# Two normalised tiles per batch go from VectorE to ScalarE in the two routers of an audio tower

## The reference

```python
def _layernorm(x, axis=-1, eps=1e-05):
    m = jnp.mean(x, axis=axis, keepdims=True)
    v = jnp.var(x, axis=axis, keepdims=True)
    return (x - m) / jnp.sqrt(v + eps)
# first mixture
S = jax.nn.softmax(x @ Wg, axis=-1)          # x = layernorm(h), Wg 128 x 8
# second mixture
logits = t @ gate_w.T + gate_b
probs = jax.nn.softmax(logits, axis=-1)
h = h + _L0_ffn_ref(_layernorm(h, axis=-1), ...)
h = h + _L1_ffn_ref(_layernorm(h, axis=-1), ...)
```

## Time and profile before

| what | value |
|---|---|
| median of 3 runs | 3237.22 us (3235.11 to 3238.65) |
| profiled execution | 3239.33 us |
| its span | 3237.6 us |
| busy PE, DVE, ACT, POOL | 2806.1, 2397.2, 1872.4, 1005.0 us |
| mean granted TensorE clock | 0.932 of full speed |

### The profile page before, as it was taken

How to read it: one execution, slowest core, us unless ns; L and a number is a source line. 1 busy time by engine, 2 the same in 40 slices (tenths; PEclk the granted TensorE clock), 3 DMA queues, 4 the chain that set the end, 5 groups by cost and what they waited for, 6 DMA issues and landing times. The chain is left out here.

```text
span 3237.6 us, 56270 instructions
## 1 busy us (share of the span) xinstructions
PE 2806.1 (87%) x16922; PEld 2239.5 (69%) x16922; DVE 2397.2 (74%) x4399; ACT 1872.4 (58%) x3098; POOL 1005.0 (31%) x873
## 2 busy tenths in 40 slices
PE   8975999999999999419999999588855899799994
PEld 8975665665666665319999999488844688688883
DVE  4544888888888886778999999377738666578775
ACT  3343466666666666308888888144422677577773
POOL 0033000000000000204555555233302577466664
PEclk9988899999999999759999999699967899899997
DMA  1138444355344341002322222220040211277767
GB/s 51 33 141 275 60 67 61 49 64 62 51 60 65 52 56 23 27 15 77 91 84 86 85 86 90 88 99 0 0 169 2 89 48 48 91 239 245 241 192 228
DMA packets 149262, 290.48 MB, mean 90 GB/s; under 512 B 23006, under 2 KB 77981, under 8 KB 142220
## 3 DMA queue, kind: packets, MB, share of 16 engines
q1 hardware_dynamic: 135564, 264.13, 33.4%
q0 software_dynamic: 13568, 24.75, 2.3%
HBM read 203.15 MB, written 87.11 MB: 90 GB/s over the span
## 5 line engine op out<-in xcount | busy, mean ns | idle before, releaser
L840 DVE TENSOR_REDUCE part_max<-to_dve 128x1 f32<-128x374 f32 (+1 forms) x1536 | 744.0, 540 | 163.3 <-PE to_dve L750 148.6
L902 ACT ACTIVATE probs<-score 128x748 f32<-128x748 f32 x768 | 579.7, 794 | 403.9 <-PE score L770 402.5
L750 PE MATMUL to_dve<-k_stack,q_stack 127*128 127x374 f32 (+1 forms) x1536 | 509.7, 377 | 30.9 <-DMA k_stack<-k_parts 30.8
L750 PEld LDWEIGHTS to_dve<-k_stack,q_stack 127*128 127x128 f32 (+1 forms) x1536 | 272.7, 190 | 299.6 <-DVE part_max L840 252.4
L2460 DVE TENSOR_TENSOR m_hid_lo<-m_hid,m_hid_hi 128x512 fp32r<-128x512 f32 x408 | 289.8, 711 | 161.3 <-ACT m_hid_hi L2433 161.3
L770 PE MATMUL score<-q_stack,k_stack 128*128 128x374 f32 x1536 | 395.1, 339 | 0.0
L1357 DVE TENSOR_TENSOR f_hid_lo_c<-f_hid_c,f_hid_hi_c 128x748 fp32r<-128x748 f32 x256 | 350.0, 1376 | 42.6 <-ACT f_hid_hi_c L1340 39.6
L680 POOL TENSOR_TENSOR h<-h,o_rows 128x256 f32 (+2 forms) x96 | 49.4, 531 | 944.9 <-DVE o_rows L863 944.9
L1253 POOL TENSOR_TENSOR f_acc_c<-f_acc_c,f_gate_c 128x748 f32<-128x748 f32 x112 | 253.1, 2259 | 259.6 <-DVE f_gate_c L1373 259.3
L786 PE MATMUL o_sum<-probs,v_sb 128*17 128x374 f32 (+1 forms) x3072 | 315.9, 483 | 16.4 <-ACT o_cols L893 14.0
L1335 ACT ACTIVATE f_hid_c<-f_up_c,c_b 128x374 f32<-128x374 f32 x512 | 268.5, 571 | 76.3 <-DVE f_hid_lo_c L1357 52.0
(11 more groups left out here) (412 smaller groups left out, 6170.9 us busy)
## 6 DMA issues: line engine op xcount, KB each, us to landing
m_weights<-e_records SPq DMA_DIRECT2D x54, 1028.0 KB, 6.8
f_gate_c<-c_gates SPq DMA_DIRECT2D x128, 374.0 KB, 3.4
q_stack<-q_parts SPq DMA_DIRECT2D x128, 187.0 KB, 5.4
k_stack<-k_parts SPq DMA_DIRECT2D x128, 187.0 KB, 9.4
e_slots<-blank SPq DMA_DIRECT2D x54, 260.0 KB, 3.6
m_row_in<-e_slots SPq DMA_DIRECT2D x54, 260.0 KB, 3.0
m_weights<-e_sums SPq DMA_DIRECT2D x16, 640.0 KB
e_records<-rec_parts SPq DMA_DIRECT2D x16, 512.0 KB, 3.9
```

What stands on the lines that cost most here:

```text
L750: last = pe.matmul(ring[bank][0:ROWS[c], 0:HALF], q_stack[its_slot][0:MAX_ROW, head, c * P:c * P + ROWS[c]], k_stack[its_slot][0:MAX_ROW, ...
L840: dve.tensor_reduce(part_max[0:ROWS[c], head, c, half:half + 1], ring[bank][0:ROWS[c], 0:HALF], AX.X, ALU.max).then_inc(used, 1)
L902: act.activation(probs[:, s % 2, head, :, :], score[e % 2][:, :, 0:HALF], ACT.Exp).then_inc(prob_done, 1)
```

## The change

`OWN`, the number of tiles per batch that DVE normalises, goes from 4 to 2. ScalarE makes tiles 2 and 3 with one `activation` of kind Identity each, whose scale is the token's `rstd` and whose bias is a new `shift` = -mean * rstd. The `shift` of all 96 tiles is one more DVE instruction at the end of `weights_and_statistics` (L205), in all four calls. PE's `turn_rows(b)` has one wait more, for `act_ready`. POOL's part is as before.

```diff
@@ weights_and_statistics, DVE
-                dve.reciprocal(g.rstd[:, :], std[:, :])
+                dve.reciprocal(g.rstd[:, :], std[:, :]).then_inc(sums_done, 1)
+                dve.wait_ge(sums_done, 4)
+                dve.scalar_tensor_tensor(out=g.shift[:, :], in0=g.mean[:, :], scalar=-1.0, in1=g.rstd[:, :],
+                                         op0=ALU.mult, op1=ALU.mult)
@@ router_logits
-        OWN = 4
-        centred, pool_ready = sem("r_centred"), sem("r_pool_ready")
+        OWN, SHIFTED = 2, 4
+        centred, pool_ready, act_ready = sem("r_centred"), sem("r_pool_ready"), sem("r_act_ready")
...
-                    tiles = slice(b * TILES + OWN, (b + 1) * TILES)
-                    out = rows_of(b)[:, OWN:TILES, :]
+                    tiles = slice(b * TILES + SHIFTED, (b + 1) * TILES)
+                    out = rows_of(b)[:, SHIFTED:TILES, :]
...
                 def turn_rows(b):
                     pe.wait_ge(ready, b + 1)
                     pe.wait_ge(pool_ready, b + 1)
+                    pe.wait_ge(act_ready, b + 1)
...
             @block.scalar
             def _(act):
+                def norm(b):
+                    if b >= 2 and keep is None:
+                        act.wait_ge(turned, b - 1)
+                    for c in range(OWN, SHIFTED):
+                        at = b * TILES + c
+                        last = act.activation(rows_of(b)[:, c, :], g.h[:, at, :], ACT.Identity,
+                                              bias=g.shift[:, at:at + 1], scale=g.rstd[:, at:at + 1])
+                    last.then_inc(act_ready, 1)
+
+                norm(0)
+                norm(1)
                 for b in range(B):
                     act.wait_ge(turned, b + 1)
                     if b >= 2:
                         act.wait_ge(done, b - 1)
                     round_cols(act, y_hi[:, b % 2, :], turn[b % 2]).then_inc(rounded, 1)
+                    if b < B - 2:
+                        norm(b + 2)
```

More of the change, by code:

```diff
@@ L956, in _ @@
                         pool.wait_ge(turned, b - 1)
-                    tiles = slice(b * TILES + OWN, (b + 1) * TILES)
-                    out = rows_of(b)[:, OWN:TILES, :]
+                    tiles = slice(b * TILES + SHIFTED, (b + 1) * TILES)
+                    out = rows_of(b)[:, SHIFTED:TILES, :]
                     pool.tensor_tensor(out, g.h[:, tiles, :], g.mean[:, tiles].unsqueeze(2).broadcast_to(
-                        [P, TILES - OWN, P]), ALU.subtract).then_inc(centred, 1)
+                        [P, TILES - SHIFTED, P]), ALU.subtract).then_inc(centred, 1)
                     pool.wait_ge(centred, b + 1)
-                    pool.tensor_tensor(out, out, g.rstd[:, tiles].unsqueeze(2).broadcast_to([P, TILES - OWN, P]),
+                    pool.tensor_tensor(out, out, g.rstd[:, tiles].unsqueeze(2).broadcast_to([P, TILES - SHIFTED, P]),
                                        ALU.mult).then_inc(pool_ready, 1)
@@ L2557, in audio_tower @@
         g.rstd = ctx.enter_context(nc.sbuf_tensor("rstd", [P, B * TILES], F32))
+        g.shift = ctx.enter_context(nc.sbuf_tensor("shift", [P, B * TILES], F32))
         g.stats = ctx.enter_context(nc.sbuf_tensor("stats", [P, B * TILES, 6], F32))
```

## The result

The change makes the kernel faster by 0.28%: 3227.60 us is the median of 12 runs (3224.76 to 3229.71) against 3235.93 us of 12 runs of the kernel before (3233.57 to 3238.71); the ratio is 0.9972, 95% interval 0.9965 to 0.9980, so 6.5 to 11.3 us less. The forecast was 3227.5 us. That the two agree to 0.1 us is partly luck: the forecast took 9.7 us from a median of 3237.22, which three runs gave, and twelve runs of the same kernel have 3235.93; the medians differ by 8.3 us.

A forecast was written before the change was run, and what follows sets the result against it. DVE, its norms held up by POOL, was taken to bound the routers, with a 1.94 us loop behind it. The terms -7.2 - 3.7 + 1.2 = -9.7 us, against 3237.22, gave 3227.5 us, range 3225.2 to 3231.6.

The forecast's parts named there:

- What bounds it: Both routers: DVE sets the pace, 2.667 us a batch in router c, its norms held up by POOL's instructions.
- A loop of 1.94 us: Routers, behind DVE: two batches through PE, ScalarE and DVE take 3.88 us, so no period under 1.94.
- four pieces: The loop's 3.88 us: split to PE 1.06, transposes 0.84, rounding 0.88, the rest 1.10 for the matmuls.
- Router c, -7.2 us: Router c: with two norms on DVE, periods of 1.95 us from batch 4 on; last split 7.2 us earlier.
- Router e, -3.7 us: Router e: periods of 2.05 us while POOL works, then 1.95; 3.7 us less, bounds 3.0 to 4.1.
- The shift, +1.2 us: Four statistics blocks: one more DVE instruction on the path, 0.3 us each, 1.2 us more (0.9 to 1.6).
- ScalarE's work at nothing: Both routers: two activations per batch, 0.45 us each, fall where ScalarE idles and cost nothing.
- The limit of 1.09 us for the activations: Routers: ScalarE's next rounding comes late only once the pair of activations takes 1.09 us (1.94 - 0.85).
- Rival 1: Both routers: POOL's hold-ups stay and DVE remains the bound, period 2.23; -5.7 us, 3231.5 us; 14%.
- Rival 2: Routers: ScalarE takes DVE's place if a pair exceeds 1.09 us; at 0.9 for one, 3238.4 us; 5%.
- Rivals 3 and 4: Routers: PE's clock falls, 3261 us, 2%; or the loop gives way too, -11 to -12.5 us, 5%.
- rival 4: Routers: the fast clock may come a batch earlier, or waits shorten, -11 to -12.5 us; 5%.

The follow-up runs named there:

- c_no_pool_before: Kernel before, with POOL leaving out its two tiles in router c from batch 2 on; router c 38.7 us, router e 42.9 us.
- c_no_pool_after: Changed kernel, with POOL leaving out its tiles in router c from batch 2 on; router c 39.7 us, periods 1.70 and 2.21 in turn.
- ring3: Changed kernel with three buffers, norms of batch b+3 behind batch b, PE's transposes of b+2 ahead of matmuls of b; routers 34.2 and 35.6 us.
- after_again: Changed kernel itself, unchanged, timed again on another chip; ratio 0.9968 to the kernel before, routers 39.2 and 38.8 us.
- own1: Changed kernel with one tile per batch on DVE and three on ScalarE; routers 38.2 and 38.6 us.
- own0: Changed kernel with no tile on DVE and all four on ScalarE; routers 41.7 and 41.6 us, period 2.27 us.
- own3: Changed kernel with three tiles on DVE and one on ScalarE; routers 44.1 and 41.1 us, period 2.41 us in router c.
- late_clear: Changed kernel with POOL's five clears moved behind its first two batches; both routers 37.7 us.

## Why the prediction was right, point by point

*What bounds it.* DVE, lengthened by hold-ups, in front: confirmed by `c_no_pool_before` (1.95 with four norms). A loop of 1.94 us behind it: confirmed by `c_no_pool_after` (3.91 for two batches, DVE idle in both, without any hold-up) and `ring3` (1.72 when the loop is opened). The prediction read 3.88 us for two batches; measured 3.91. Of its four pieces the last, 1.10 for the matmuls, was only what was left over, so that they add up is no test.

*Router c, -7.2 us.* Measured -7.86. The eleven periods behind batch 4 were 1.95 each as forecast. The rest is in the first four batches: `split` of batch 4 stood 14.8 us into the router, and the forecast had 15.4. The fast clock came earlier. PE's matmuls of the changed kernel at the change of levels:

```profile
1349.02 0.51 PE L987 MATMUL r_sums_c<-r_hi_c,c_wg_lo 128*128 128x374 f32 x1
1349.33 1.35 PE L212 MATMUL r_turn_c<-ident,r_rows_c 128*128 128x128 f32 x6
1350.46 0.41 PE L987 MATMUL r_sums_c<-r_hi_c,c_wg_hi 128*128 128x374 f32 x1
1350.71 0.33 PE L987 MATMUL r_sums_c<-r_lo_c,c_wg_hi 128*128 128x374 f32 x1
```

The last slow matmul (0.51 us) starts 8.1 us into the router; before it was at 1350.00, 11.3 us in. This is no property of the change that I can show: in `after_again`, the same kernel, the last slow matmul starts 11.0 us in, `split` of batch 3 came at 13.2 us instead of 12.9 and that of batch 4 at 15.4 as forecast, and router c took 39.2 us instead of 38.6. Against 46.4 that is the forecast's 7.2 less; so the 0.7 us more of the first trace look like scatter.

*Router e, -3.7 us.* Measured -4.04. The step that was off is the period beside a working POOL, 2.05 forecast and 1.95 measured: from batch 3 on two norms there took 0.89 to 1.04 us, not 1.14, and the loop hides that. (The bound of -4.1 for 1.94 throughout should read -4.2: 2452.2 + 12 x 1.94 = 2475.5.) `split` of batch 3 came 12.9 us into the router as worked out (2452.2 - 2439.3).

*The shift, +1.2 us.* Measured 4 x 0.29: 0.26 and 0.03 for the wait. What the added semaphore costs, put at under 0.1 us, no run shows.

*ScalarE's work at nothing.* The activation takes 0.48 to 0.51 us (32 in each router) and a pair 0.89; forecast 0.45 and 0.9. The estimate from the Trainium skill (ScalarE: Activation LUTs, What ACT_TABLE_LOAD costs), 0.48 and 0.87, agrees with the trace. The limit of 1.09 us for the activations was too low: it took the rounding's duration, 0.85, where the step is 0.73. `own1` with 1.27 us for three (a step of 1.17) still fits into 3.91 for two; `own0`, with a step of 1.55, does not.

*Rival 1* was right that one norm is still held up in every batch of router c beside POOL, and wrong that it matters at two tiles while the loop is closed; at three it does (`own3`), and at two with the loop opened (`ring3`, router e). *Rival 2* is what `own0` shows. *Rivals 3 and 4*: the mean clock of the routers is 0.88 and 0.87, as in the earlier trace rows; nothing fell. The earlier rise of the clock in router c looks like rival 4, but `after_again` does not repeat it.

## What to carry to other kernels

Before moving work off the busiest engine, ask why its instructions take as long as they do. Here 1.76 us a batch for four norms was 1.04 of work and 0.72 of waiting for POOL, and taking POOL's share away gave the same gain as taking half of DVE's. The next limit could be read from the trace of before, in a stretch where the first one is absent: the end of router c, without POOL and without a norm in front of `split`, gave the 1.94 us at which both routers now run. When a period alternates while the sum of two stays, and every engine has idle time, look for a loop over two buffers; alternation alone is not enough, since router e before (3.09 and 3.22) and in `ring3` (1.84 and 1.96) alternates with DVE busy throughout beside a POOL that never pauses. A third buffer, another order on PE and later clears together were worth 9.3 us, nearly as much again as the change itself (10.5 on that chip).

## What the runs showed of the hardware

- A hold-up goes by POOL's instructions, not by DVE's: of two, three or four norms beside two POOL instructions one or two were stretched, while POOL's own had medians of 0.61 to 0.64 us in every run and never more than 0.70. It need not end with one instruction of POOL: in `late_clear` one norm was stretched to 2.00 us while POOL ran a multiplication and five clears with no gap between them.
- An engine's durations overlap at the ends: two norms of together 0.89 us take 0.80 from the start of the first to the next instruction, and four activations of 1.68 us take 1.55. Sums of a period need steps, not durations.
- The rise of the granted clock after an idle stretch moved by some 3 us between executions of router c that do the same at the start (the last slow matmul starts 8.1, 11.0 and 11.3 us in, in the first trace of the changed kernel, `after_again` and `c_no_pool_after`). It goes with their lengths, 38.6, 39.2 and 39.7 us at one and the same pace.
